# The tail's layer norm is scaled by GpSimd instead of VectorE

## The reference, cut to what matters

```
def _layernorm(x, axis=-1, eps=1e-05):
    m = jnp.mean(x, axis=axis, keepdims=True)
    v = jnp.var(x, axis=axis, keepdims=True)
    return (x - m) / jnp.sqrt(v + eps)
...
    x = x + 0.5 * _L0_ffn_ref(_layernorm(x, axis=-1), ...)
    x = x + _L0_attn_ref(_layernorm(x, axis=-1), ...)
    x = x + 0.5 * _L0_ffn_ref(_layernorm(x, axis=-1), ...)
    x = x + 0.5 * _L1_ffn_ref(_layernorm(x, axis=-1), ...)
    x = x + _L1_attn_ref(_layernorm(x, axis=-1), ...)
    x = x + 0.5 * _L1_ffn_ref(_layernorm(x, axis=-1), ...)
```

## Time and profile before

| | us |
|---|---|
| median of 3 runs | 2860.79 |
| lowest, highest run | 2854.37, 2863.7 |
| the profiled execution | 2854.86 |
| its span in the profile | 2853.1 |
| busy in the span: TensorE / VectorE / ScalarE / GpSimd | 2595.9 / 1841.9 / 1228.5 / 747.9 |
| mean granted clock of TensorE | 0.946 |

### The profile page before, as it was taken

How to read it: one execution, slowest core, us unless ns; L and a number is a source line. 1 busy time by engine, 2 the same in 40 slices (tenths; PEclk the granted TensorE clock), 3 DMA queues, 4 the chain that set the end, 5 groups by cost and what they waited for, 6 DMA issues and landing times.

```text
span 2853.1 us, 45542 instructions
## 1 busy us (share of the span) xinstructions
PE 2595.9 (91%) x15278; PEld 1723.8 (60%) x15278; DVE 1841.9 (65%) x5524; ACT 1228.5 (43%) x2805; POOL 747.9 (26%) x1285
## 2 busy tenths in 40 slices
PE   5875899989999999999999999999999999998996
PEld 4663566556656666566655666566665666655644
DVE  4454666776667667676676766776667766776642
ACT  2321244454444444444444444454444444444452
POOL 2421222223222232223322232222222233221111
PEclk8996899999999999999999999999999999999998
DMA  2024013411334112422145113332134221343311
GB/s 61 1 68 119 18 24 75 128 39 30 72 88 108 41 43 64 130 64 58 24 110 131 37 32 72 94 102 54 29 79 124 55 58 36 103 112 74 80 31 48
DMA packets 135248, 193.93 MB, mean 68 GB/s; under 512 B 46239, under 2 KB 108014, under 8 KB 124654
## 3 DMA queue, kind: packets, MB, share of 16 engines
q1 hardware_dynamic: 133440, 190.89, 26.4%
q10 hardware_dynamic: 1582, 0.13, 0.0%
HBM read 122.29 MB, written 67.63 MB: 67 GB/s over the span
## 4 chain that ended last, share of the span: by engine, by line
PE 71%; DVE 16%; issue 2%; ACT 2%; POOL 1%; DMA 1%; SPq 0%; DVEq 0%; ACTq 0%; POOLq 0%
PE bank L798 10%; PE bank L817 9%; PE bank L783 9%; PE bank L620 4%; PE bank L711 4%; DVE bank L1137 4%; PE bank L551 4%; PE bank L569 4%; PE bank L600 3%; PE bank L560 3%; PE bank L725 3%; PE bank L530 3%; PE bank L712 2%; PE bank L655 2%; PE bank L768 2%
## 5 line engine op out<-in xcount | busy, mean ns | idle before, releaser
L1343 ACT ACTIVATE pexp<-bank 128x512 f32<-128x512 f32 (+3 forms) x1536 | 677.3, 499 | 575.4 <-PE bank L798 575.2
L1137 DVE CUSTOM_DVE_ANT_0 bank<-bank,maskneg 128x256 f32<-128x256 f32 (+3 forms) x1024 | 484.1, 511 | 263.0 <-PE bank L783 258.9
L798 PE MATMUL bank<-stq,stk 128*128 128x512 f32 (+3 forms) x1536 | 547.5, 427 | 30.9 <-ACT pexp L1343 24.1
L783 PE MATMUL bank<-stk,stq 128*128 128x512 f32 (+3 forms) x1536 | 506.4, 394 | 62.5 <-DVE mxa L1137 24.6
L798 PEld LDWEIGHTS bank<-stq,stk 128*128 128x128 f32 x1536 | 267.9, 195 | 320.1 <-ACT pexp L1343 190.5
L1140 DVE TENSOR_REDUCE mxa<-bank 128x1 f32<-128x512 f32 x512 | 345.8, 683 | 146.5 <-PE bank L783 142.3
L1497 POOL TENSOR_SCALAR_AFFINE_SELECT pexp<-pexp 128x256 f32<-128x256 f32 x512 | 212.4, 422 | 763.6 <-ACT pexp L1343 763.4
L783 PEld LDWEIGHTS bank<-stk,stq 128*128 128x128 f32 x1536 | 281.5, 198 | 174.4 <-issue 136.0
L817 PE MATMUL bank<-pexp,vsm 128*32 128x512 f32 (+3 forms) x3072 | 343.8, 521 | 20.1 <-POOL pexp L1497 19.9
L1409 POOL TENSOR_SCALAR_AFFINE_SELECT arena<-arena 128x512 f32<-128x512 f32 x128 | 78.2, 634 | 393.4 <-ACT arena L1245 393.3
L530 PE MATMUL bank<-ident,arena 128*128 128x128 f32 x768 | 117.9, 301 | 46.7 <-DVE arena L861 42.6
(11 more groups left out here) (186 smaller groups left out, 4051.6 us busy)
## 6 DMA issues: line engine op xcount, KB each, us to landing
stq<-q_halves SPq DMA_DIRECT2D x128, 256.0 KB
arena<-rope_table SPq DMA_DIRECT2D x16, 1024.0 KB
q_halves<-arena SPq DMA_DIRECT2D x32, 512.0 KB, 2.8
k_halves<-arena SPq DMA_DIRECT2D x32, 512.0 KB, 2.9
stk<-k_halves SPq DMA_DIRECT2D x64, 256.0 KB
stk<-k_halves SPq DMA_DIRECT2D x128, 128.0 KB
v_rows<-arena SPq DMA_DIRECT2D x16, 544.0 KB, 4.1
vsm<-v_rows SPq DMA_DIRECT2D x16, 544.0 KB, 3.8
```

The lines of the kernel that those rows point to most:

```text
L783: last = mm(bk[:, col:col + n], stq[b_][:, h % 2, qb * P:(qb + 1) * P], stk[b_][:, h % 2, k0:k0 + n], start=True, stop=True)
L798: mm(ps(j)[:, 0:n], stk[b_][:, j, kb * P:(kb + 1) * P], stq[b_][:, j, (c + 1) * CH - n:(c + 1) * CH], start=True, stop=True).then_inc(s["t ...
L1137: last = nc.vector.tensor_tensor_reduce(out=sc, in0=sc, in1=maskneg[:, CH - n:CH], scale=1.0, scalar=LOWEST, op0=ALU.add, op1=ALU.max, acc ...
L1343: nc.scalar.activation(pexp[:, u % NPX, j, 0:n], ps(j)[:, 0:n], ACT.Exp, scale=DK ** -0.5).then_inc(s["exp_done"], 1)
```

## The change

For the tail (q >= NC, where NC is 2) the four scalings leave VectorE with their two waits. GpSimd issues the same four operations directly behind the root, in the same tick, after a wait for that root on its own semaphore. The front's norms stay as they are. Nobody else's waits are changed: the transposes still wait for four counts of `xn`.

```diff
--- before.py
+++ after.py
@@ -855,9 +855,10 @@
                         nc.vector.bn_aggr(mv[:, q, t], stats[:, q, t]).then_inc(s["ln"][q], 1)
                     yield
                     yield
-                    nc.vector.wait_ge(s["ln"][q], 8 * norms(q, b, n) + 8)
-                    nc.vector.wait_ge(s["rs"][q], 2 * norms(q, b, n) + 2)
-                    for t in range(4):
+                    if q < NC:
+                        nc.vector.wait_ge(s["ln"][q], 8 * norms(q, b, n) + 8)
+                        nc.vector.wait_ge(s["rs"][q], 2 * norms(q, b, n) + 2)
+                    for t in range(4 if q < NC else 0):
                         nc.vector.tensor_scalar(dst[:, t], xs[:, t], mv[:, q, t, 0:1], rstd[:, q, t:t + 1], ALU.subtract,
                                                 ALU.mult).then_inc(s["xn"][q], 1)
                     yield
@@ -1360,6 +1361,12 @@
                     nc.gpsimd.tensor_scalar(varep[:, q], mv[:, q, :, 1], EPS, None, ALU.add).then_inc(s["rs"][q], 1)
                     nc.gpsimd.wait_ge(s["rs"][q], 2 * norms(q, b, n) + 1)
                     nc.gpsimd.tensor_tensor(rstd[:, q], varep[:, q], mhalf[:], ALU.pow).then_inc(s["rs"][q], 1)
+                    if q >= NC:
+                        xs, dst = xq(q), xnsG[q - NC]
+                        nc.gpsimd.wait_ge(s["rs"][q], 2 * norms(q, b, n) + 2)
+                        for t in range(4):
+                            nc.gpsimd.tensor_scalar(dst[:, t], xs[:, t], mv[:, q, t, 0:1], rstd[:, q, t:t + 1], ALU.subtract,
+                                                    ALU.mult).then_inc(s["xn"][q], 1)
                     yield
                     yield from idle(3)
```

## The result

Thirteen runs of each gave a median of 2864.7 us (2860.47 to 2874.19) for the changed kernel and 2857.96 us (2851.06 to 2863.7) for the one before. The ratio is 1.0032, with a 95% interval of 1.0019 to 1.0045: slower by 5 to 13 us. I had forecast 1.3 us faster. The profiled executions stand in the same relation: a span of 2859.8 against 2853.1 us, 6.7 us more.

What follows compares the result with a forecast made beforehand. The prediction took TensorE, busy 91% of the span, to bound the kernel. Its terms, 0 - 1.6 - 0.3 + 0.6 = -1.3 us, took the median of 2860.79 us to 2859.5 us, with a range of 2853 to 2866.

Steps and rivals of the forecast that it cites:

- What it adds: 64 scalings on GpSimd, taken at 555 ns each; the norm ready 2.3 us after the root.
- the scalings take over 1 us each: One of the signs that the prediction named for being wrong, about the price of GpSimd's scalings.
- bound from above: Upper limit for one GpSimd scaling: 1812 ns, the longest run of a TENSOR_SCALAR twice as wide.
- Rival (b): GpSimd's scalings are slow, taking turns with VectorE: at 1.1 us 2864 us, at 1.81 us 2877 us; chance 0.12 in all.
- Collisions: In the steady tails, q=2's first scaling meets a VectorE instruction and would start a few tenths of a us late.
- Five steady tails: Tails of batches 0 to 4: cost nothing and give nothing, covered by TensorE's own queue.
- Batch 5: TensorE's 1.76 us wait for a maximum shrinks to 0.2 us: 1.6 us saved.
- rival (a): In batch 5 the clock stays at 2.4 GHz once the wait goes, giving 2856.1 us; chance 0.20.
- Batch 6: Wait for a maximum goes, selects behind q=3's scalings come late: of 1.4 us, 0.3 us gain is left.
- The last tail: End of the program: q=3's norm 0.8 us later, its root 0.2 us earlier; cost 0.6 us.
- Sum: All tails together: 0 - 1.6 - 0.3 + 0.6 = -1.3 us, forecast 2859.5 us.

Runs made afterwards that it cites:

- e2_early: GpSimd scales the tail norms in batches 0 to 4 only, VectorE in 5, 6 and 7; ratio 1.0000 to the kernel before.
- e8_double: GpSimd scales in batches 0 to 4 only and does the four scalings twice; ratio 1.0087 to the kernel before.
- e4_muladd: All sixteen tail norms on GpSimd, written mult-then-add with two small instructions behind the root; ratio 1.0011 to the kernel before.
- e5_addmult: All sixteen tail norms on GpSimd, written add-then-mult with the mean negated ahead of the root; ratio 1.0001 to the kernel before.
- e3_late: VectorE scales the tail norms in batches 0 to 4, GpSimd in 5, 6 and 7; ratio 1.0022 to the kernel before.

## Why the prediction was wrong, point by point

- **What it adds: the step that failed.** "I take 555 ns, the same operation, size and kind of operands." The instruction was the same, the two operations inside it were not: L1394 is mult-then-add, the tail's scaling subtract-then-mult. It measured 1219 ns, and "the scalings take over 1 us each" was my own first sign of being wrong. I had matched on name, shape and operands, and the rows of the profile don't print the operations; the source lines do. My own bound from above (1812 ns) held, but I gave it to collisions and weighed it at 0.12. Rival (b) was near in its price (1.1 us) and right in its sign, and wrong in its reason. That its 2864 us lies so near the measured 2864.7 is luck in part: it starts from a median of 2860.79 where thirteen runs gave 2857.96, and its terms (-1.6, +1.8, +2.8) aren't those of the traces (-3.8, +4.1, +4.8). The median lies in my range of 2853 to 2866 too, near its upper end, and the forecast's working didn't lead there.
- **Collisions.** They exist and are small: 1.44 and 1.90 us for two of the four scalings of q=2 in the steady tails, no more in the bare ones. The Trainium skill, page "SBUF — State Buffer", section "Who interferes with whom", says that a VectorE instruction with two SBUF inputs contends with a GpSimd instruction that reads SBUF. The trace agrees: L886 has two SBUF inputs, and the two longer scalings are those beside it. The Trainium skill, page "GPSIMD Engine Reference", section "Engine selection", calls one-input work on GpSimd roughly line-rate. For this pair of operations the measured 1219 ns against VectorE's 422 contradict that, for mult-add 559 ns come nearer to it.
- **Five steady tails: right.** No cost, no gain; e2_early bears it out with 1.0000 and no wait for a norm. The margins that I gave were too wide, since 4.9 to 5.7 us went into them and not 2.3.
- **Batch 5: right in kind, its size open.** 1.6 us was for VectorE's relief, and that wait did shrink. The drop of the clock around the 1.76 us wait, rival (a), went with it: the sixteen L696 take 1.91 us instead of 3.55. But that execution had an early and long drop (6.8 us); e2_early and e8_double, with the same wait, have one of 3.4 us and are themselves 1.3 and 3.1 us ahead of it. The kernels with the slow scaling are 2.1 to 3.8 us ahead, so a gain from them isn't shown; those with the fast one, 4.3 to 6.3 us, lie clear of both.
- **Batch 6: wrong by the price.** Forecast -0.3 us, by way of q=3's selects alone. With the slow form 2.7 to 4.1 us were lost, 1.9 of it by the start of q=2's transposes, a norm that I hadn't priced here (the wait of 2.16 us), and a part of the rest at the lower clock behind them. With the fast form it was 0.3 and 0.5: q=2's wait is gone, but the one for a select is 1.77 us in e4_muladd and 1.35 in e5_addmult, where I had said about 1. So even at the right price the gain was not there.
- **The last tail: wrong by the price, and by the path.** Forecast 0.6 us, measured 4.8 (4.6 in e3_late). Four scalings at 1219 ns are 2.7 us dearer than at 555. And I had let q=2's delay go, since "q=3's come five microseconds later and are last". It was the other way round: 3.4 of the 4.8 us are the longer wait for q=2 (3.83 against 0.42), and the wait for q=3 shrank from 1.60 to 0.21, because the product between them ran at 1.2 GHz. The clock stood in no term of this tail. At the fast price it is still 2.5 us, with no wait for q=3 at all.
- **Sum.** In single executions: batch 5 -3.8, batch 6 +4.1, last tail +4.8 is 5.1 of the 6.7 us; the rest (1.6 us) lies where executions differ anyway. With the price that I had assumed, e5_addmult, the kernel is level with the one before.

## What to carry to other kernels

Before a step goes to GpSimd, look up a row there with the same pair of operations, not only the same instruction and shape, and if there is none, time the form by itself: subtract-then-mult cost 1219 ns where add-then-mult cost 559, and a negated mean buys the fast one for 0.23 us. Work that is moved off the bounding engine's path is free only while it fits the cover (here 0.8 us were left, and 4.9 us more cost 4.0 us each time), and the place that has no cover, the end of the program, cost most in the trace (4.8 us). There, follow every norm to the end and not only the last one, and look at what now queues behind the moved work on its new engine.

## What the runs showed of the hardware that I had not expected

- GpSimd's TENSOR_SCALAR with two operations falls into two prices, 0.84 ns an element for mult-add and 3.33 for subtract-mult; the two pairs with a subtract that were tried are in the dear one. With one operation instead of two and an operand from SBUF it is slower (924 to 927 ns) than with add and mult together (559 ns).
- The wait of 1.76 us on TensorE in batch 5 went with a drop to 1.2 GHz in all three kernels that have it: in the one before it began 0.5 us ahead of the wait's end and lasted 6.8 us, in e2_early and e8_double it began 1.7 and 1.8 us after the end and lasted 3.4. In the six where GpSimd scaled there, the wait was 0.59 us or 0.12 and no drop began within 15 us of it. In the last tail a norm of q=2 that came 0.9 to 3.4 us later (waits of 1.34, 1.76 and 3.83 us against 0.42) went with 6.8 us more at the lower clock.
